# Preparing the second pair among the first pair's maxima in three attentions, and the first attention's keys and queries ahead of the last two trees' outputs

## The reference, cut to what matters

```python
x = x + _L0_xattn_ref(_layernorm(x), ctx, ctx, ...)   # linear attention
x = x + _L0_ffn_ref(_layernorm(x), W_in, b_in, W_out) # eight trees of 255 nodes
x = x + _L1_xattn_ref(ctx, ctx, _layernorm(x), mask, Wv, Wk, Wq)    # 16 heads
x = x + _L1_ffn_ref(...)                              # quantised, with a convolution
x = x + _L2_xattn_ref(_layernorm(x), ctx, ctx, mask, wq, bq, ...)   # 16 heads
x = x + _L2_ffn_ref(...)                              # ternary weights, gated
x = x + _L3_xattn_ref(_layernorm(x), ctx, ctx, Wqkv, ..., 32)       # 32 heads
x = x + _L3_ffn_ref(...)                              # eight experts, one per token
```

## Time and profile before

| | |
|---|---|
| median of 3 runs | 1598.71 us (1598.57 to 1599.04) |
| the profiled execution | 1599.02 us, its span 1597.3 us |
| PE busy | 1445.9 us, 91% of the span |
| DVE busy | 1085.4 us, 68% |
| ACT busy | 774.6 us, 48% |
| POOL busy | 128.8 us, 8% |
| mean granted clock of PE | 0.962 of full speed |

### The profile page before, as it was taken

The page is one execution under the profiler, slowest core; times in us unless marked ns, Lnnn a source line. Parts: engine busy times, 40 slices in busy tenths (PEclk is TensorE's granted clock), DMA queues, the critical chain, the costliest instruction groups (busy, mean ns, idle before and its releaser), DMA issues.

```text
span 1597.3 us, 26924 instructions
## 1 busy us (share of the span) xinstructions
PE 1445.9 (91%) x9942; PEld 1088.4 (68%) x9949; DVE 1085.4 (68%) x2390; ACT 774.6 (48%) x1336; POOL 128.8 (8%) x184
## 2 busy tenths in 40 slices
PE   6999999968887999798989999999997989899788
PEld 5666666647774445477786878777773767778677
DVE  4455566678887777787866465554548989887555
ACT  2212112257774576576672132222223977777666
POOL 1000000000000000111000000000002010002344
PEclk9999999989998999999998999999998999999899
DMA  9462202140000000000007900000100000004122
GB/s 322 159 230 79 79 1 79 56 160 14 14 2 1 1 1 1 25 14 1 14 2 254 334 1 1 0 1 0 33 0 7 8 8 1 8 1 133 62 79 71
DMA packets 59120, 90.29 MB, mean 57 GB/s; under 512 B 11199, under 2 KB 50621, under 8 KB 58686
## 3 DMA queue, kind: packets, MB, share of 16 engines
q1 hardware_dynamic: 56238, 72.14, 13.9%
q10 hardware_dynamic: 544, 12.16, 2.3%
q0 software_dynamic: 2208, 4.27, 0.8%
HBM read 65.09 MB, written 36.82 MB: 64 GB/s over the span
## 4 chain that ended last, share of the span: by engine, by line
PE 55%; issue 17%; DVE 15%; ACT 5%; DVEq 5%; POOL 1%; ACTq 1%; POOLq 1%; another core or an unknown queue 0%; DMA 0%
PE bank L2235 8%; PE bank L2236 8%; PE bank L1815 7%; PE bank L1793 7%; DVE MB L1046 3%; DVE plo L1064 3%; PE bank L1980 3%; PE bank L1866 2%; PE bank L1721 2%; PE bank L1875 1%; PE bank L1951 1%; PE bank L2033 1%; PE bank L1985 1%; PE bank L1953 1%; PE bank L1984 1%
## 5 line engine op out<-in xcount | busy, mean ns | idle before, releaser
L1064 DVE TENSOR_TENSOR plo<-e,phi 120x512 f16<-120x512 f32 x256 | 180.2, 709 | 46.5 <-ACT phi L1551 42.6
L1545 ACT ACTIVATE e<-bank 120x512 f32<-120x512 f32 x256 | 150.6, 588 | 55.4 <-PE bank L1985 45.4
L1551 ACT ACTIVATE phi<-e 120x512 f16<-120x512 f32 x256 | 161.2, 630 | 10.1 <-PE bank L2012 1.5
L1046 DVE TENSOR_REDUCE MB<-bank 128x4 bf16<-128x480 f32 x256 | 155.9, 648 | 11.4 <-PE bank L1953 8.1
L1446 ACT ACTIVATE act<-bank,bin 127x512 f32<-127x512 f32 x64 | 43.0, 686 | 167.3 <-DVE dec L801 163.3
L1793 PE MATMUL bank<-xT,winT 128*127 128x512 f32 (+1 forms) x256 | 114.6, 593 | 1.3 <-ACTq L1417 1.3
L1815 PE MATMUL bank<-woutT,msk 128*128 128x256 f32 (+1 forms) x512 | 115.1, 379 | 0.0
L720 DVE TENSOR_SCALAR high<-raw 128x512 int32<-128x512 int32 x96 | 41.0, 427 | 107.9 <-ACT raw L1702 60.9
L578 POOL TENSOR_TENSOR veps<-mv,ceps 128x4 f32<-128x4 f32 x32 | 8.8, 276 | 1301.8 <-DVEq L691 1170.0
L1815 PEld LDWEIGHTS bank<-woutT,msk 128*128 128x128 f32 (+1 forms) x512 | 96.9, 190 | 15.4
L2235 PE MATMUL bank<-hah,h1w 128*128 128x512 f32 x256 | 101.3, 396 | 3.3 <-DVE hal L723 3.3
(11 more groups left out here) (309 smaller groups left out, 3594.4 us busy)
## 6 DMA issues: line engine op xcount, KB each, us to landing
copy_routed<-zeros SPq DMA_DIRECT2D x1, 18744.0 KB, 70.5
seen<-in_h1T SPq DMA_DIRECT2D x8, 512.0 KB, 7.2
seen<-in_h2T SPq DMA_DIRECT2D x8, 512.0 KB, 5.1
h1w<-copy_h1T SPq DMA_DIRECT2D x1, 4096.0 KB, 16.7
h2w<-copy_h2T SPq DMA_DIRECT2D x1, 4096.0 KB, 14.7
jx<-copy_routed SPq DMA_DIRECT2D x30, 132.0 KB
ctxp<-in_ctxT SPq DMA_DIRECT2D x13, 240.0 KB, 2.7
m<-in_mask SPq DMA_DIRECT2D x9, 240.0 KB, 2.9
```

Of the source, the lines that this page charges most:

```text
L1046: dve.tensor_reduce(MB[:, t, h0 // 8, SK + h0 % 8:SK + h0 % 8 + 4], b[:, 0:4 * SK].rearrange("p (h k) -> p h k", h=4), AX.X, ALU.max).then ...
L1064: dve.tensor_tensor(plo[:, g % 3, :], e32[:, g % 3, :], phi[:, g % 3, :], ALU.subtract).then_inc(s.lo, 1)
L1545: act.activation(e32[:, g % 3, :], bank[2 + g % 3][0:SK, :], ACT.Exp).then_inc(s.exp, 1)
L1551: act.activation(phi[:, g % 3, :], e32[:, g % 3, :], ACT.Copy).then_inc(s.phi, 1)
```

## The change

1. **All three attentions.** The second pair's preparation no longer stands behind all of the first pair's maxima. With `i = -1`: `norm_stats` for pair 1 comes on DVE right after pair 0's low queries (ahead of the first `maxima`), the normed rows on ACT at `u` 3 (ahead of pair 0's `low_keys`), `keys(1)` at `u` 6 (8 with 32 heads), the transposed rows at `u` 8 (11), both in the banks `AHEAD_BANK` and the one after it. `values_in(1)` and `value_rows(1)` move into pair 0's loop, at its units 2 and 4. `mask(1)` stays in `u` `n-2`. In the second attention the first scores wait for the copied rows, since they share bank 2.
2. **The last pair of the trees.** PE transposes the rows into banks 4 and 5, then runs the first attention's `keys(0)`, `values_in(0)` and both `queries(0, f)` (banks 2 and 3 now), and only then the outputs of trees 6 and 7. DVE adds the trees' output to `x` at `u` 5 of the first attention. Its low bits are taken at trees 3, 4 and 5 instead of 3, 5 and 7. `keys(1)` (banks 0 and 1) waits for that addition.
3. **SP** loads the first mask, the next mask and the next context before it waits for `res_done`, and so ahead of the 7.3 MB.

```diff
-QUERY_BANKS = {"l1x": (5, 6), "l2x": (0, 1), "l3x": (5, 6)}
+QUERY_BANKS = {"l1x": (2, 3), "l2x": (0, 1), "l3x": (5, 6)}
+AHEAD_BANK = {"l1x": 0, "l2x": 2, "l3x": 0}
...
+        self.keyed0, self.columned0 = (6, 8) if heads == 16 else (8, 11)
...
+            if L is L1X:
+                sp.dma_start(m32[:], a["mask"][0:TOK, :].rearrange("(t p) k -> p t k", p=128)).then_inc(mask_ready, 16)
+                next_loads(0)
             sp.wait_ge(res_done, 4 * L.phase + 1)
...
+            with sp.Fori(1 if L is L1X else 0, PAIRS) as i:
+                next_loads(i)
...
-                    for q in ((), (), (), (0, 1), (), (2, 3), (), (4, 5))[p]:
+                    for q in ((), (), (), (0, 1), (2, 3) if i == PAIRS - 1 else (),
+                              (4, 5) if i == PAIRS - 1 else (2, 3), (), () if i == PAIRS - 1 else (4, 5))[p]:
...
+                if i < PAIRS - 1:
+                    tree_residual(i)
...
-            if L is L1X:
-                dve.wait_ge(res_done, 4 * ph + 1)
...
+                if step == 2 - n:
+                    dve.wait_ge(ln_rstd, 4 * ph + 1)
+                    norm_stats(ph, 0)
                 if ahead:
                     for m in range(L.tiles(u - 1), L.tiles(u)):
                         maxima(i + 1, m)
...
+                if i == 0 and u == 4:
+                    value_rows(1)
+                if L is L1X and i < 0 and u == L.split:
+                    tree_residual(PAIRS - 1)
+                elif ahead and u == L.split:
                     split_values(i + 1)
...
-            if L is not L1X:
-                act.wait_ge(bias_done, 1)
+            act.wait_ge(wrcp if L is L1X else bias_done, 1)
...
+                if i < 0 and u == 3:
+                    norm_rows(4 * ph + 2)
+                if i < 0 and u == L.keyed0:
+                    keys(1)
+                if i < 0 and u == L.columned0:
+                    evacuate_xT(4 * ph + 2, AHEAD_BANK[L.name])
...
+                elif L is L2X and g == 0:
+                    pe.wait_ge(xT_ready, 4 * ph + 2)
...
             if L is L1X:
-                pe.wait_ge(res_done, 4 * ph + 1)
+                keys(0)
                 pe.wait_ge(xT_ready, 4 * ph + 1)
-                keys(0)
                 values_in(0)
+                pe.wait_ge(s.k32, 1)
+                for f in range(K2):
+                    queries(0, f)
+                leaf_rows(PAIRS - 1, TREES - 2)
+                leaf_rows(PAIRS - 1, TREES - 1)
...
+                if i < 0 and u == L.keyed0:
+                    if L is not L3X:
+                        pe.wait_ge(res_done, 4 * ph + 1)
+                    keys(1)
+                if i < 0 and u == L.columned0:
+                    pe.wait_ge(s.k32, L.c0 + 2)
+                    transpose_rows(4 * ph + 2, AHEAD_BANK[L.name])
+                if i == 0 and u == 2:
+                    values_in(1)
-                if 1 <= i + 2 < PAIRS and u == L.keyed:
+                if 2 <= i + 2 < PAIRS and u == L.keyed:
                     keys(i + 2)
```

More of the change, by code:

```diff
@@ L780, in _, with tree_residual @@
                 dve.drain().then_inc(res_done, 1)
+        def tree_residual(i):
+            dve.wait_ge(Bf.out, i + 1)
+            for h in range(2):
+                residual(i, h, bank[h][:, :])
+            dve.drain().then_inc(res_done, 1)
         if phases > 1:
@@ L821, in _ @@
                 masked(TREES - 1)
-                dve.wait_ge(Bf.out, i + 1)
-                for h in range(2):
-                    residual(i, h, bank[h][:, :])
-                dve.drain().then_inc(res_done, 1)
+                if i < PAIRS - 1:
+                    tree_residual(i)
             dve.tensor_reduce(lowall[:], lowmax[:], AX.X, ALU.max)
@@ L1163, in attention @@
                     low_queries(i + 1, u - 1)
+                if L is L1X and step == 2 - n:
+                    split_values(0)
                 if L is L2X and step == 2 - n:
@@ L1175, in attention @@
                     divide(sg)
-                if ahead and u == L.split:
+                if i == 0 and u == 4:
[3 more added lines that the diff above has]
+                elif ahead and u == L.split:
                     split_values(i + 1)
@@ L1771, in _, with leaf_rows @@
                 transpose_rows(i + 2)
+        def leaf_rows(i, p):
+            for c, n in ((0, INNER), (1, LEAVES)):
+                pe.wait_ge(Bf.msk, i * (2 * TREES) + (2 * p + c + 1))
+                for t in range(TT):
+                    last = pe.matmul(bank[t // 2][:, (t % 2) * D:(t % 2) * D + D],
+                                     msk0[0:n, p % 2, c, tok(t)], woutT[0:n, 2 * p + c, :],
+                                     start=(p == 0 and c == 0 and t % 2 == 0),
+                                     stop=(p == TREES - 1 and c == 1), skip_group_check=True)
+            if p == TREES - 1:
+                last.then_inc(Bf.out, 1)
         if phases > 1:
@@ L1810, in _ @@
                         pe.wait_ge(res_done, i + (4 + 1))
[L1811 to L1819 removed]
+                    if 0 <= p < (TREES if i < PAIRS - 1 else TREES - 2):
+                        leaf_rows(i, p)
         def gate_logits(p):
```

64 lines of the change are left out of this document (29 added, 35 removed).

## The result

The changed kernel takes 1577.24 us (median of 4 runs, 1572.39 to 1579.12) against 1598.64 us before (1595.03 to 1599.04, 4 runs on the same chip): a ratio of 0.9869, 95% interval 0.9844 to 0.9895. The forecast was 1576.4. The profiled execution took 1575.43 us with a span of 1573.7 us and a mean granted clock of 0.967. Two later executions that stand far outside their groups (6563.95 us of the changed kernel, 1702.65 us of the one with the context last) are left out of all medians and ratios.

The account below looks back on a forecast made before the run. The prediction saw a relay bounding each attention's start, with every later exponential hanging on the first. Gains of 14.4, 3.8 and 4.1 us took 1599.02 to 1576.7 for the profiled execution, median 1576.4, range 1568 to 1587.

Parts of the forecast that it names:

- the sum: All three attentions: gains of 14.4, 3.8 and 4.1 us, 22.3 together, giving 1576.7 us for the profiled execution; chance 0.58.
- First attention: Tree outputs beside DVE's list and a shorter tail: first exponential at 333.2, 15.2 us earlier; 14.4 net, bounds 10 to 17.
- the two stops: First attention, among pair 0's maxima: waits for the tree addition and the copied keys, costing 1.2 and 1.4 us on PE.
- Second: Second attention: first exponential at 668.2, 4.4 us earlier; 3.8 net after the loop's terms, bounds 1 to 6.5.
- Third: Third attention: first exponential at 1234.0, 6.2 us earlier; 4.1 net after the loop's terms, bounds -1 to 8.
- The loops of pair 0: Behind each first exponential: `value_rows(1)` puts 0.65 us on DVE at unit 4 in the first attention, plus small slips.
- SP's loads, "cost nothing": SP's three loads moved ahead of 7.3 MB of weights, and those moved behind the tree addition, cost nothing.
- B: Second and third attention: new waits replace the old, so only the first attention's 14 us remain, 1585.0; chance 0.16.
- C: All attentions: the stops hide and DVE catches up in the loops, 29 us gained, 1570.0; chance 0.14.
- D: Second and third attention: POOL's addition locks out DVE's cast, 1.8 us lost each, gain 18.7, 1580.3; chance 0.06.
- E: Pair 0's loops: new stops leave PE at 1.2 GHz, 1.8 us a unit lost; 1613 at 20 units; chance 0.03.
- F: Normed rows come late on ACT, low keys and tiles wait, the tail only changes place: 1599; chance 0.03.

Follow-up runs that it names:

- the one with the context last: The changed kernel, but SP issues the first attention's second mask and context behind the tables, as before: 1589.77 us, ratio 1.0012.
- the trees' tail alone: The changed kernel with pair 1's preparation put back behind pair 0's maxima in all three attentions: 1589.38 us, ratio 0.9942; again 1588.85 us, 0.9936.
- pair 1's preparation with the context first: The kernel before with pair 1's preparation moved and the second mask and context issued ahead of the tables: 1568.55 us, ratio 0.9894; again 1582.81 us, 0.9893.
- pair 1's preparation alone: The kernel before with only pair 1's preparation moved among pair 0's maxima; trees and SP's queue as before: 1588.23 us, ratio 0.9936.
- the moved split: The changed kernel with the split of pair 0's values right behind pair 1's statistics in all attentions: 1568.75 us, ratio 0.9889.

## Why the prediction was right

**The total** was 1576.4 against 1577.2, and the sum for the profiled execution 1576.7 against 1575.4. The mechanism was right where it was tested: both halves gain where the sum puts them, at the start of the attentions. That the totals agree within 1.3 us is in part luck, since the three profiled executions of the changed kernel give 23.3, 22.1 and 20.2 us at the last attention's pair 3, and their parts vary more (see The result). The terms, judged one by one on the first:

**First attention, 14.4 predicted, 13.4 measured** (14.6 at the first exponential, against 15.2). Tree outputs end at 316.31 (315.8 expected), low queries at 315.28 (314.7), the first maximum starts at 318.87 (318.05), the addition ends at 323.53 (322.9), the copied keys at 327.07 (326.7), the exponential starts at 333.84 (333.2). The chain runs 0.4 to 0.8 late throughout. It starts 0.35 late at the masked product (ends 305.05 instead of 304.7), because PE's last path counts end at 303.60 and not "unchanged" at 303.27; the rest is gaps between DVE's small instructions that the sum did not carry. Of the two stops, the one for the tree addition was 1.07 (1.2 expected) and the one for the copied keys 0.36. The sum holds about 0.9 for the latter (four maxima from 325.25, then on at 328.4), while its bounds call it 1.4. It came out smaller mostly because DVE got there 0.7 late. In the second execution the keys ran at the lower level and the first stop was 2.76: the 1.7 us for the keys hold only at the full level.

**Second, 3.8 predicted, 3.3 measured.** From the end of the additions to the first exponential there are 18.78 us instead of 23.08: 4.3, against 4.4. (The terms as written add up to 4.9, not 4.4: 662.1 plus 4.3 is 666.4, and with the 1.35 of the first attention the exponential would stand at 667.7.) But the step to the first exponential shows only 3.0, because the convolution layer before it took 1.3 us longer in this execution (182.07 against 180.74 from the last attention's mark, 20.5 us at the lower clock against 13.7). That layer is unchanged, and the trees' tail alone shows 182.08 as well, while the repeats of the changed kernel show 180.41 and 182.05. The loop then gave 0.3 back where I had taken 0.6 off.

**Third, 4.1 predicted, 6.5 measured**, and 3.9 and 4.4 in the other two executions. The first exponential came 6.2 earlier, as predicted to the tenth, but with different parts. The two stops of DVE sum to 4.2, where the sum has 4.1 for PE's keys and 0.5 for ACT's copied keys; they were 2.3 and 1.9, and 0.4 and 4.0 in the second execution. The keys were priced at 5.0 us and took 4.03, 3.40 and 3.61: the 5.45 of the kernel before was already a mixture of both levels. What held DVE was ACT's list, which the sum put at 0.5. So the size was right for a partly wrong reason. Behind it I took off 2.1 for DVE's longer series and `value_rows`; pair 0's loop grew by 0.9 and pair 1's shrank by 1.2. In the other two executions pair 0's loop grew by 2.0, as predicted. The shrinking is not the change's: pair 1's loop takes 72.11 us at a granted clock of 0.95 in the kernel before and 70.88 at 1.00 here, and with the trees' tail alone, where that loop is the old one, 71.56 at 0.98 and 72.10 at 0.95.

**The loops of pair 0.** I priced `value_rows(1)` at 0.65 in each, plus smaller slips. The clock moves these loops by more than that with one and the same code. The windows of the first attention's loop in the first and in the second execution of pair 1's preparation with the context first:

```profile
340.20:379.00 38.80, 34.66 (x433) 28.68 (x432) 33.73 (x76) 30.26 (x56) 2.34 (x4) 1.00 0.10 27
```

```profile
340.00:380.40 40.40, 37.29 (x433) 30.37 (x433) 33.56 (x76) 30.31 (x54) 2.33 (x4) 0.93 0.10 26
```

DVE's busy time is the same. So loops can be compared only at the same granted clock. In the second attention that can be done: here is its loop in the changed kernel, and then with the trees' tail alone, which has the old loop:

```profile
656.23:699.03 42.80, 39.79 (x444) 31.98 (x443) 35.36 (x76) 31.09 (x54) 4.79 (x5) 1.00 0.09 25
```

```profile
666.60:707.70 41.10, 37.70 (x435) 30.46 (x434) 33.20 (x72) 30.97 (x55) 4.79 (x5) 1.00 0.05 14
```

The repeats agree (42.79 and 42.82; 41.10). The work that moved into this loop costs it 1.7 us at the full level; I had taken off 0.6, 0.5 and given 0.5 back. In the third attention, at 0.97, it is 68.7 us with pair 1's preparation alone against 67.5 in the kernel before: 1.2, where I had 2.1. In the first, at 0.94, it is 40.37 (the changed kernel's second execution) against 39.36: 1.0, where I had 0.8. The granted clock has two digits here, so these are good to a few tenths. That the changed kernel still came out no worse in the second attention's loop (42.8 against 43.14) is the clock's doing, 0.95 in the one execution of the kernel before.

**SP's loads, "cost nothing".** True of the tables, and this is the prediction's real omission: the moved context was priced as something that might do harm, not as something that the rest needs. Without it the change is worth nothing that can be measured (ratio 1.0012, 0.9999 to 1.0025).

**The rivals.** B and C were the bounds and did not come. D's mechanism did come, in one of its two places: the cast met POOL's addition in the second attention (2.66 us for the two casts, in the repeats as well). Of its price of 1.8 an estimated 0.8 at most lay on the path, as said above. The Trainium skill, SBUF — State Buffer, section "Who interferes with whom", says that whoever issues first holds the shared pair for the whole instruction while the other is blocked, and that `tensor_reduce` never contends. The trace agrees: the longer of the two casts took 2.45 us instead of 0.29 and ended 0.15 after the addition, and the reductions of the third attention beside the addition took 0.65 to 0.66, as elsewhere. E, the lower clock, came as a matter of 1 to 2.5 us a loop in some executions, far from 1.8 us a unit. F is refuted: the tail from the last copied tile to the first exponential is 1.5 us. The table load is hidden, and the exponential starts 1.49 after it begins (1.30 in the other two attentions), so the row was the right price and not the 2.66 us of the Trainium skill, ScalarE: Activation LUTs, section "What ACT_TABLE_LOAD costs".

## What to carry to other kernels

Where a pipeline's first round ends in a serial tail (statistics, reciprocal, rows, transposes, table load), weave the second round's preparation into the first: with that half alone the three stages gave 8.2, 4.3 and 4.2 us at the first exponential for an unchanged amount of work, of which pair 0's loop behind took 1 to 1.7 back at equal clock. When a consumer moves earlier, follow each of its inputs back to the queue that loads it, and look how early it lands now; a small load behind 7.3 MB on one queue undid all of it. An engine that is slowed while it would have waited anyway has lost little. Where two waits follow each other, cutting the first only lengthens the second until the list behind the second is cut too. And compare loops at the same granted clock before you call a difference the change's.

## What the runs showed of the hardware

A small load issued behind four large ones was held at the issue, not only in transfer: SP spent 9.76 and 9.49 us in issuing a mask of 240 KB that takes 0.38 elsewhere, 9.53 in the kernel before, and 4.46 in the changed kernel, where it starts 5.8 us after the last table's issue. The context then landed 7.4 to 7.5 us after its issue, against a median of 2.8 on the page.

How long the lower level lasts behind an idle stretch of PE doesn't follow from that stretch. In the second attention's tail PE idled 5.01 us in two executions of the changed kernel, and the clock was at the lower level for 3.4 us in the one (to 643.6) and 6.8 in the other (638.0 to 644.8); behind 6.51 us with the moved split it was 6.8. The two tails of the changed kernel were equal all the same (18.78 and 18.77).

The same kernel takes up to 2.5 us more or less in one loop (42.81 at a granted clock of 1.00 and 45.32 at 0.95, pair 0 of the second attention with the context first). The spans of three executions of the changed kernel were 1573.7 to 1576.7.

One of the three chips takes 12 us less for the kernel before, and 14 less for pair 1's preparation with the context first. In the four profiles from it 138.9 to 139.0 us lie behind pair 3's first exponential of the third attention, where the expert layer is, against 149 to 152 in the ten others. In one of the slower ones PE and its weight loads wait 8.8 us there for rows to be normed (`jxln`), but in the kernel before, with 151.6 us, only 0.3, so that isn't the cause. It stays open.
